# LayerNorm, causal squared-score attention and a gated 8-expert mix on 8 cores: LayerNorm and final-stage loads issued from ScalarE's queue, one addition moved to GpSimd

## The reference, cut to what matters

```python
# x: (4, 4096, 1024) f32; 16 heads of 64; 8 experts, top 2
xn = layernorm(x)
q = rope(rmsnorm(xn @ Wq.T + bq)); k = rope(rmsnorm(xn @ Wk.T + bk)); v = xn @ Wv.T + bv
scores  = einsum('bqhd,bkhd->bhqk', q, k)
pattern = square(scores / 64) * causal            # no softmax
z = einsum('bhqk,bkhd->bqhd', pattern, v)
s = xn + z @ Wo.T
logits = xn @ gate_w.T + gate_b                   # top 2 of 8 kept, softmax over them
e = einsum over experts of softmax * (xn @ expert_w + expert_b)
out = x + s * silu(e)
```

## Time and profile before

| | |
|---|---|
| two runs | 2384.44 and 2450.83 us, median 2417.63 us |
| the profiled execution | 2386.54 us, span of its slowest core 2385.0 us |
| spans of the 8 cores | 2366.1 to 2385.0 us |
| VectorE, ScalarE, GpSimd busy | 1068.5, 767.5 and 470.0 us (45%, 32%, 20%) |
| TensorE busy | 1698.1 us (71%) |
| mean granted TensorE clock by core | 0.713 to 0.729 |

### The profile page before, as it was taken

The page is one execution under the profiler, slowest core; times in us unless marked ns, Lnnn a source line. Parts: engine busy times, 40 slices in busy tenths (PEclk is TensorE's granted clock), DMA queues, the critical chain, the costliest instruction groups (busy, mean ns, idle before and its releaser), DMA issues.

```text
span 2385.0 us, 24513 instructions; the slowest of 8 cores (2366.1 to 2385.0 us)
## 1 busy us (share of the span) xinstructions
PE 1698.1 (71%) x6768; PEld 571.2 (24%) x6768; DVE 1068.5 (45%) x1636; ACT 767.5 (32%) x914; POOL 470.0 (20%) x322
## 2 busy tenths in 40 slices
PE   0120778787787888888887878887459778688685
PEld 0000233333331111111111111123123333233232
DVE  2111665566654555454545454542354343343333
ACT  1001444554454555555555555551000000000000
POOL 1000445554451111111111111110000200300203
PEclk9665788988885555555555555559679988899898
DMA  9997222233352101010111100016313333333342
GB/s 186 122 115 114 86 98 89 71 104 118 118 109 77 45 14 43 14 40 23 34 27 29 27 27 7 20 39 214 115 36 131 113 110 126 113 114 133 115 141 106
DMA packets 148559, 200.44 MB, mean 84 GB/s; under 512 B 59720, under 2 KB 97608, under 8 KB 147920
## 3 DMA queue, kind: packets, MB, share of 16 engines
q1 hardware_dynamic: 142560, 173.68, 22.6%
q0 software_dynamic: 5872, 25.20, 8.6%
HBM read 173.72 MB, written 67.11 MB: 101 GB/s over the span
## 4 chain that ended last, share of the span: by engine, by line
PE 37%; DMA 22%; DVE 15%; issue 9%; ACT 7%; SPq 4%; POOL 3%; another core or an unknown queue 3%; DVEq 0%; ACTq 0%; POOLq 0%
PE p L973 9%; PE p L722 9%; PE p L776 9%; DMA s_abf<-webf 7%; DMA s_af<-x 7%; ACT s_abf L736 5%; PE p L423 4%; DVE s_abf L741 4%; DVE s_abf L751 3%; PE p L620 2%; DMA vsp<-s_abf 2%; PE p L825 2%; POOL s_af L1022 1%; SPq L958 1%
## 5 line engine op out<-in xcount | busy, mean ns | idle before, releaser
L736 ACT ACTIVATE s_abf<-p 128x1024 bf16<-128x1024 f32 x480 | 491.1, 1023 | 415.6 <-PE p L776 400.1
L973 PE MATMUL p<-s_abf 128*128 128x512 bf16 x2048 | 485.1, 399 | 124.7 <-DVE s_af L987 79.4
L722 PE MATMUL p<-s_abf 64*128 64x512 bf16 x1280 | 389.7, 595 | 128.1 <-DVE s_abf L741 45.0
L776 PE MATMUL p<-s_abf 128*64 128x512 bf16 x1280 | 407.7, 632 | 35.0 <-DVE s_abf L797 33.0
L987 DVE SCALAR_TENSOR_TENSOR s_af<-p,s_g_all,s_af 128x512 f32<-128x512 f32 x256 | 180.2, 746 | 284.0 <-PE p L973 279.5
L973 PEld LDWEIGHTS p<-s_abf 128*128 128x128 bf16 x2048 | 204.1, 102 | 398.7 <-issue 190.3
L745 POOL TENSOR_TENSOR s_abf<-s_abf 128x1024 bf16<-128x1024 bf16 x80 | 151.4, 1892 | 749.7 <-DVE s_abf L741 749.7
L761 DVE TENSOR_TENSOR s_abf<-s_abf,s_masks 128x1024 bf16<-128x1024 bf16 x256 | 173.6, 701 | 185.5 <-POOL s_abf L745 103.0
L423 PE MATMUL p<-s_abf 128*128 128x512 bf16 x768 | 193.7, 406 | 16.2 <-DVE s_af L460 13.6
L620 PE MATMUL p<-s_abf 128*128 128x512 bf16 x512 | 138.8, 420 | 79.0 <-DVE s_tiny L541 38.6
L722 PEld LDWEIGHTS p<-s_abf 64*128 64x128 bf16 x1280 | 80.1, 100 | 426.9 <-issue 426.9
(11 more groups left out here) (73 smaller groups left out, 1085.7 us busy)
## 6 DMA issues: line engine op xcount, KB each, us to landing
s_abf<-webf SPq DMA_DIRECT2D x104, 512.0 KB, 5.8
s_af<-x SPq DMA_DIRECT2D x48, 512.0 KB, 4.0
webf<-we POOLq DMA_DIRECT2D x8, 2048.0 KB, 77.5
vsp<-s_abf SPq DMA_DIRECT2D x32, 256.0 KB, 2.1
xnsp<-s_abf SPq DMA_DIRECT2D x64, 128.0 KB, 1.8
ksp<-s_abf SPq DMA_DIRECT2D x8, 1024.0 KB, 4.6
s_abf<-ksp SPq DMA_DIRECT2D x64, 128.0 KB, 2.5
s_abf<-vsp SPq DMA_DIRECT2D x32, 256.0 KB, 3.1
```

Source lines behind the costliest of these rows:

```text
L722: _sp=sp, _ws=wsl: E.matmul(_sp[:, _u * QG:(_u + 1) * QG], kT_w[_ws].ap(_kb * 128, (_kb + 1) * 128, 64 * _u, 64 * _u + 64), qT_sl[_sl].ap( ...
L736: E.activation(_pat.ap(0, 2 * QG), _sp[:, 0:2 * QG], AF.Square),
L776: (lambda E, _u=u: E.matmul(p01[64 * _u:64 * _u + 64, _u * QG:(_u + 1) * QG], v_w[_ws].ap(_kb * 128 + _u * 64, _kb * 128 + _u * 64 + 64), ...
L973: _pp=pf[pi0 + half], _s=esl: E.matmul(_pp[:, 0:HW], xnT_dh.ap(_ki * SO + _rc * 128, _ki * SO + (_rc + 1) * 128), we_r[_s].ap(_ki * D + _h ...
```

## The change

Four things change. The 1 MB load of the masks at the start is issued from ScalarE's queue instead of SyncE's. So are the x loads of the odd LayerNorm tiles (slot 1, 16 loads), and all 32 loads of the final steps (sdram and x rows). The addition srow += xnrow (L1018, 16 of them) goes from VectorE to GpSimd. In the changed kernel everything from L526 on stands one line later, so L533 is L534 there, and L1018 is L1019.

```diff
-        ld("sync", masks[:, :].rearrange("p (c m q) -> p c m q", c=2, m=NQB),
+        ld("scalar", masks[:, :].rearrange("p (c m q) -> p c m q", c=2, m=NQB),
...
-                ops.append(("sync", [lambda E, _rc=rc, _sl=sl: E.dma_start(
-                    out=xbuf[_sl].view(),
-                    in_=x_d[_rc * 128:(_rc + 1) * 128, :])],
+                ops.append(("sync" if sl == 0 else "scalar",
+                    [lambda E, _rc=rc, _sl=sl: E.dma_start(
+                        out=xbuf[_sl].view(),
+                        in_=x_d[_rc * 128:(_rc + 1) * 128, :])],
...
-                b.op("sync", lambda E, _sl=sl, _rc=rc: E.dma_start(
+                b.op("scalar", lambda E, _sl=sl, _rc=rc: E.dma_start(
                     out=srow[_sl].view(),
...
-                b.op("sync", lambda E, _sl=sl, _rc=rc: E.dma_start(
+                b.op("scalar", lambda E, _sl=sl, _rc=rc: E.dma_start(
                     out=xrow[_sl].view(),
...
-                b.op("vector", lambda E, _sl=sl: E.tensor_tensor(
+                b.op("gpsimd", lambda E, _sl=sl: E.tensor_tensor(
                     srow[_sl].view(), srow[_sl].view(), xnrow.view(),
                     ALU.add),
```

## The result

The changed kernel takes 2484.01 us at the median of its runs (2473.95 to 2533.05) against 2390.14 for the kernel before: ratio 1.0411, 95% interval 1.0379 to 1.0443, so it is slower by 4.1% (94 us between the medians, 98 by the ratio). The forecast was 2410 with a range of 2365 to 2440. In some executions the cores of one die run at a lower clock and longer, whatever the kernel; the ratios leave these out, and the one profile that fell there (e7) gives no number here.

What follows compares the result with a forecast made beforehand. TensorE had 37% of the chain that ended last, DMA 22%, VectorE 15%, with x loads 7%. The terms -6 + 12 + 5 - 3 + 12 + 3 = +23 on the profiled 2386.5 gave 2410 us, range 2365 to 2440.

Steps and rivals of the forecast that it cites:

- The start: 0 to 235 us: expert weight copies keep DMA engines 0.95 busy and end at about 222 either way; -6 us.
- LayerNorm loads: Projection stage, 235 to 695 us: VectorE waits for odd tiles' loads, +3 a pair at five pairs, less 3; +12 us.
- two waits of VectorE per pair: Sign that the forecast is right: VectorE waits twice per LayerNorm pair for x, first about 5 us.
- Into the attention: Attention's start: ScalarE's square held +11 us behind a final-stage x row load, half taken as covered; +5 us.
- Out projection: VectorE's 6.75 us sdram wait goes with the addition; ScalarE issues loads between its evacuations; -3 us.
- Ends of groups: Three ends of expert groups: normalisation stands one pair earlier while the x row comes no earlier; +4 each, +12 us.
- Tail: Last step: slower GpSimd addition and one more cold tile behind the last normalisation, less the saved wait; +3 us.
- Rival (c): Five pairs, attention's start and three group ends: ScalarE as issuer is held by each load; 2449 us, chance 0.17.
- (a): Rival, whole kernel: loads are hidden anyway and the terms cancel; 2388 us (2375 to 2396), chance 0.24.
- (b): Rival, the start: odd tiles' own queue brings the sixth tile with the fifth, later terms at half; 2357 us, chance 0.09.
- a span more than 48 us off with the attention stage itself longer: Sign that the forecast is wrong: span more than 48 us off with the attention stage itself longer or shorter.

Runs made afterwards that it cites:

- e7: Kernel before with only the addition moved to GpSimd, all loads on SyncE; gave no ratio, repeated as e12.
- e3: Kernel before with only the odd LayerNorm loads on ScalarE's queue, plainly scheduled: ratio 1.0206, first scores at 739 us.
- e9: e3 with square and sum of tiles 3, 7, ... 31 scheduled behind the normalisation of the tile before: ratio 0.9994, first scores at 697 us.
- e1: Kernel before's order in every list, but all moved loads emitted on ScalarE and the addition on GpSimd: ratio 1.0002.
- e10: Kernel before with one VectorE instruction moved, tile 0's final-step normalisation in front of the attention's first cast: ratio 1.0063.
- e11: Kernel before with ten VectorE normalisations at the ends of expert groups moved one pair, one bias copy or both earlier: ratio 1.0081.
- e2: Changed kernel's order in every list, but all moved loads emitted on SyncE and the addition on VectorE: ratio 1.0464.
- e6: Kernel before with only the final stage's 32 loads on ScalarE, addition left on VectorE: ratio 1.021, experts 631 us.
- e12: Kernel before with only the addition on GpSimd, a repeat of e7: ratio 0.999, experts 595.5 us in the median core.
- e5: e3 with the sum of tiles 3, 7, ... 31 scheduled behind the normalisation of the tile before: ratio 1.0125, first scores at 726 us.
- e13: Kernel before's order, only odd LayerNorm loads emitted on ScalarE and the addition on GpSimd; masks and final loads on SyncE: ratio 0.9975.
- e14: e9 with the addition on GpSimd too, plainly scheduled, against the kernel before: ratio 0.9955, 2383.71 us.

## Why the prediction was wrong

The direction was right and the size was not: +23 forecast, about +94 to +98 measured. By its own steps:

- **The start, -6.** The eighth tile's sum came 1.1 us earlier (229.5 against 230.6), the sixth at 157.6 us where it had come at 145.3. That the end of the start hardly moves was right. But the later sixth tile says nothing of its queue: its load went out only at 110.45, once its buffer was free, and took 47 us to land, where it had gone out at 70.62 and taken 75.

```profile
110.45 0.33 ACTq L527 DMA_DIRECT2D s_af<-x  x1
157.60 2.00 ACT L534 ACTIVATE s_af<-s_af 128x1024 f32<-128x1024 f32 x2 [49.79 <-DMA s_af<-x]
```

The rule of the Trainium skill (page "DMA: Bandwidth & Descriptors", section "Queues, rings and completion order") that engines serve queues in turn is not contradicted, and no run separates it; the time it would have given did not come.

- **LayerNorm loads, +12.** This is the step that failed: it measured +48. I had VectorE wait 5.6 us (measured 6.47) and the second sum start "at 496 + 1.2 + 5.4 = 502.6", with the even tile there when VectorE comes to it. The working never asks when that tile's load can go out. It waits for its buffer, and the normalisation that frees it was in the list I had printed, behind the new wait. My signs did name two waits of VectorE per pair, but the sum priced one. The pair costs 9 us, not 3. My upper bound (22) was made from the old waits and left a second wait of nearly the same size (3.93) out. e3 puts the loss in this edit, e9 takes 42 of 45 us of it away by order alone.
- **Into the attention, +5.** Measured +15. I priced ScalarE's hold behind the load at 11 us, half of it covered. It stood 20.73 us, as the L679 loads took 18.02 us and not 6.17, and in e1, where it is alone, it costs the stage 8 to 11 us. I did not look at VectorE's list, where the normalisation now stood in front of the first cast. e10 makes the whole loss and more (+17) with that one move.
- **Out projection, -3.** Measured -1 with the gate.
- **Ends of groups, +12.** Measured +23. The mechanism was right (the normalisation one pair earlier), the term mis-sized: I took +4 an end for the first and third step, and the fourth step of each of the first two ends moves over a pair and a bias copy, and waits 13.69 us. e11 shows +15 in the experts and +3 in the tail from the moves alone. The other 8 us are there in e2 too (634.9, all loads on SyncE), so they come with the order and not with the queue; they go with the loads' part of it (e6), and which places make them is not settled. The 0.5 us of issue in my sum and the 0.7 in its upper bound come from no row.
- **Tail, +3.** Measured +3.6.
- **The rivals.** Rival (c), ScalarE held as issuer, had the right sign and a time of 2449. But e1 and e2 show that it is not the cause: the holds at the five pairs cost nothing in the old order. I had the order rows as evidence against (a), and still gave the large loss to the queue. In (b), half of the later terms (+29) is 14.5, not 10, which changes nothing here.
- **The signs.** One that I had put under "wrong" came true: a span more than 48 us off with the attention stage itself longer (945 against 930). The 15 us lie at its start.

A normalisation was again slow beside a sum of GpSimd, 1.95 us at 1970.90 against 0.81. The Trainium skill's page "SBUF — State Buffer", section "Who interferes with whom", has this as an exclusive lock of the port pair; the rows agree. With e12 at 0.999 the 16 additions on GpSimd cost nothing here that can be measured.

## What to carry to other kernels

In a kernel whose list scheduler has a cost per engine, as this one, moving a DMA to another engine's queue is also a change of cost, and so of order; here that was the whole of the loss. Compare the lists and ask of each instruction that now waits for a load: what stands behind it that is ready, and does any of that free the buffer of the next load? Then measure order and queue apart, by scheduling as the old engine and emitting on the new one.

## What the runs showed that I had not expected

One of VectorE's 1636 instructions, in front instead of 25 us behind, costs this kernel 0.6% (e10). And a wait does not vanish when the instruction that had it is moved: in e5 it went from the sum (6.47 us) to the sum of squares (6.64 us), with 32 of e3's 45 us before the first scores.

The addition on GpSimd showed an experts' stage 16 us shorter in the median core of one execution at an unchanged time (e12). It was no accident of one execution: e13 (596.4) and e14 (590.3) have it too, while e3, e5, e9 and e10, with the addition on VectorE, lie at 605 to 615. Over the executions that its ratio counts, e13's median core has a span of 2359.1 us on average, against 2374.6 for the kernel before, and its slowest core 2381.7 against 2386.9. So the median core gains 15.5 us and the slowest, which sets the time, 5.2, which is within the noise of the ratio. What makes the median core faster is not separated by a run. A table of stages by the median core has to be read with the time of the slowest beside it.
